# Attention-and-ternary-layer kernel on eight cores: another order of the lead-in, another order in the steps without Q/K jobs, and the last tile's products in other PSUM banks

## The reference, cut to what matters

```python
xn = layernorm(x)                                  # x: 2 x 16384 x 1024, no gain or bias
q, k, v = xn @ w_q + b_q, xn @ w_k + b_k, xn @ w_v + b_v          # 16 heads of 64
scores = einsum('bhsd,bhskd->bhsk', q, k_win) / 8  # window of 7 rows around each row
attn = softmax(scores masked to valid rows)
a = einsum('bhsk,bhskd->bhsd', attn, v_win) @ w_o + b_o
scale = max(mean(|weight|), 1e-5); wt = clip(round(weight / scale), -1, 1)
out = x + a + einsum('bsi,oi->bso', xn, wt * scale)
```

## Time and profile before

| | us |
|---|---|
| median of 3 runs | 704.99 (704.03 to 753.69) |
| the profiled execution | 706.46 |
| its span on core 3, the slowest | 704.9 |
| spans of the eight cores | 695.1 to 704.9 |
| busy time of PE on core 3 | 646.4 (92% of the span) |

### The profile page before, as it was taken

How to read it: one execution, slowest core, us unless ns; L and a number is a source line. 1 busy time by engine, 2 the same in 40 slices (tenths; PEclk the granted TensorE clock), 3 DMA queues, 4 the chain that set the end, 5 groups by cost and what they waited for, 6 DMA issues and landing times.

```text
span 704.9 us, 11682 instructions; the slowest of 8 cores (695.1 to 704.9 us)
## 1 busy us (share of the span) xinstructions
PE 646.4 (92%) x3890; PEld 300.0 (43%) x3890; DVE 435.1 (62%) x533; ACT 374.7 (53%) x1418; POOL 89.0 (13%) x52
## 2 busy tenths in 40 slices
PE   1669894989999999999999999999899999999996
PEld 1234341334444444444444444444344444555542
DVE  6135579476666666666665666666666655566662
ACT  3343366355555555555555555555555555556671
POOL 1013000231111111111111111001011111111200
PEclk9989997899999999999999999999899999999998
DMA  6989975657544454566553555554453432243322
GB/s 155 214 127 326 156 123 144 128 166 180 137 126 119 127 121 128 127 127 149 129 136 90 150 135 135 135 138 117 104 95 92 110 85 80 70 135 117 91 70 81
DMA packets 129803, 91.19 MB, mean 129 GB/s; under 512 B 107856, under 2 KB 116176, under 8 KB 129744
## 3 DMA queue, kind: packets, MB, share of 16 engines
q1 hardware_dynamic: 121296, 82.05, 44.9%
q0 software_dynamic: 8448, 8.39, 8.7%
HBM read 55.82 MB, written 16.78 MB: 103 GB/s over the span
## 4 chain that ended last, share of the span: by engine, by line
PE 81%; DVE 6%; DMA 4%; ACT 4%; issue 3%; POOL 1%; SPq 0%; DVEq 0%; ACTq 0%; POOLq 0%
PE p_p L301 16%; PE p_f L457 15%; PE p_p L283 15%; PE p_f L444 15%; PE p_p L326 14%; PE p_a L414 3%; DMA wq_b<-wq 3%; PE p_s L354 3%; ACT sm L384 3%; DVE sm L369 1%; DMA x<-x 1%; DVE nmx L376 1%; DVE xr L474 1%; DVE bst L204 1%; DVE xn L225 1%
## 5 line engine op out<-in xcount | busy, mean ns | idle before, releaser
L384 ACT ACTIVATE sm<-sm,nmx 122x128 f32<-122x128 f32 x544 | 210.7, 392 | 30.1 <-DVE nmx L376 30.1
L469 POOL TENSOR_TENSOR xr<-xr,brow 128x1024 f32<-128x1024 f32 x32 | 76.7, 2399 | 522.9 <-DMA xr<-x 456.1
L283 PE MATMUL p_p<-xnt,wq_b 128*128 128x488 bf16 (+1 forms) x576 | 128.1, 370 | 7.0 <-DMA wq_b<-wq 5.8
L301 PE MATMUL p_p<-xnt,wk_b 128*128 128x494 bf16 (+1 forms) x576 | 126.0, 366 | 0.0
L326 PE MATMUL p_p<-wv_b,xnt 128*128 128x512 bf16 x544 | 124.8, 383 | 0.0
L291 ACT ACTIVATE qt<-p_p,bq 128x488 bf16<-128x488 f32 (+1 forms) x72 | 46.4, 645 | 141.9 <-PE p_p L283 141.8
L444 PE MATMUL p_f<-wft_b,xnt 128*128 128x512 bf16 x512 | 119.5, 388 | 2.2 <-DVE xr L474 2.2
L457 PE MATMUL p_f<-wo_b,att 128*128 128x512 bf16 x512 | 116.5, 379 | 0.0
L384 ACT ACTIVATION_READ_ACCUMULATOR sm<-sm,nmx 122x1 f32 x544 | 104.6, 192 | 0.0
L369 DVE TENSOR_TENSOR sm<-p_s,mk_sb 122x1024 f32<-122x1024 f32 x68 | 82.9, 1219 | 30.0 <-PE p_s L354 30.0
L339 ACT CAST v<-p_p 128x512 bf16<-128x512 f32 x68 | 39.0, 574 | 98.8 <-PE p_p L326 98.8
(11 more groups left out here) (54 smaller groups left out, 267.2 us busy)
## 6 DMA issues: line engine op xcount, KB each, us to landing
xr<-x SPq DMA_DIRECT2D x32, 512.0 KB, 4.6
out<-xr SPq DMA_DIRECT2D x32, 512.0 KB, 3.3
x<-x SPq DMA_DIRECT2D x31, 512.0 KB, 4.3
wq_b<-wq POOLq DMA_DIRECT2D x4, 512.0 KB, 11.8
wk_b<-wk POOLq DMA_DIRECT2D x4, 512.0 KB, 11.9
xr<-wft SPq DMA_DIRECT2D x4, 512.0 KB, 10.5
wv_b<-wv POOLq DMA_DIRECT2D x4, 512.0 KB, 14.8
wo_b<-wo POOLq DMA_DIRECT2D x4, 512.0 KB, 24.9
```

The lines of the kernel that those rows point to most:

```text
L283: q.do("tensor", lambda e, k=k: e.matmul(bank[:, 0:m], w_b["wq"][:, k * H + 128 * c:k * H + 128 * c + 128], rows_of(b, k, BQ * b + 3, m), ...
L301: q.do("tensor", lambda e, k=k: e.matmul(bank[:, 0:m], w_b["wk"][:, k * H + 128 * c:k * H + 128 * c + 128], rows_of(b, k, BQ * b, m), star ...
L384: q.do("scalar", lambda e, h=h: e.activation(sm[hf][0:TQ, KW * h:KW * h + KW], sm[hf][0:TQ, KW * h:KW * h + KW], AF.Exp, bias=nmx[hf][0:TQ ...
L469: q.do("gpsimd", lambda e: e.tensor_tensor(xr[t % NR][:, :], xr[t % NR][:, :], brow[:, :], ALU.add), ("xrb", t))
```

## The change

`p_t` becomes two buffers (the second in `p_f`), used in turn. w_q's half 0 is issued in two parts, one after x tile 1 and one after x tile 2, and w_q's half 1 only after tile 6, ahead of w_k. The Q jobs of columns 4 to 7 of block 0 go behind those of columns 0 to 3 of block 1. `wf_scale` and the first terns go behind `k_job(1, 1)`; the exponentials of window 0 are spread otherwise over the K jobs, and `weights(0, 1)` is written behind window 0's V jobs. In steps that aren't `qk`, `output_step` (out_add and store) comes between the two mask additions and `layer_norm_step` (normalise, DMA transpose, x load) behind them, and `exps(n, 0)` and `weights(n, 0)` come behind `att_evict(s, 0)`. In step 0 the loads of `brow` and `xr` go behind both `e_transpose`s. The last tile's products go to `p_s`, its `o_proj` finishes column half 0 four matmuls before half 1, and each half is added and stored by itself.

```diff
-        p_t = p_a[:, :].bitcast(BF16)
+        p_t = [p_a[:, :].bitcast(BF16), p_f[:, 0:512].bitcast(BF16)]
...
         def xn_by_pe(r, *blocks):
             q.need("tensor", ("xn", r), "idm")
-            if t_last:
-                q.need("tensor", t_last[-1])
+            if r >= 2:
+                q.need("tensor", t_last[r - 2])
...
+        def p_out(t):
+            return p_s if t == NO - 1 else p_f
...
         def f_proj(t):
-            if t >= 1:
+            if t == NO - 1:
+                q.need("tensor", ("sadd", NW - 1, 1))
+            elif t >= 1:
                 q.need("tensor", ("out", t - 1))
...
         def o_proj(t):
+            order = [(k, jh) for k in range(8) for jh in range(2)]
+            if t == NO - 1:
+                order = [(k, jh) for kh in range(2) for jh in range(2) for k in range(4 * kh, 4 * kh + 4)]
...
-            q.need("tensor", "wsum")
+            q.need("tensor", "wsum", t_last[7])
...
-        q.need("gpsimd", ("x", 2))
-        weight_load("wq", 0)
-        weight_load("wq", 1)
+        q.need("gpsimd", ("x", 1))
+        weight_load("wq", 0, (0,))
+        q.need("gpsimd", ("x", 2))
+        weight_load("wq", 0, (1,))
         q.need("sync", ("w", "wq", 0))
         x_load(4)
...
         q.need("gpsimd", ("x", 6))
+        weight_load("wq", 1)
         weight_load("wk", 0)
         weight_load("wk", 1)
         xn_by_pe(3, 0, 1)
-        for c in range(8):
+        for c in range(4):
             q_job(0, c)
-            if c in (3, 5, 6, 7):
-                r = {3: 4, 5: 5, 6: 6, 7: 7}[c]
-                stats(r)
-                rstd(r)
-                normalise(r)
-                if r >= 5:
-                    xn_by_pe(r - 1, 1)
+            if c >= 1:
+                stats(3 + c)
+                rstd(3 + c)
+                normalise(3 + c)
+            if c >= 2:
+                xn_by_pe(2 + c, 1)
+        stats(7)
+        rstd(7)
+        normalise(7)
+        xn_by_pe(6, 1)
         xn_by_pe(7, 1)
...
-        for c in range(8):
-            q_job(1, c)
+        for b, c in ([(1, c) for c in range(4)] + [(0, c) for c in range(4, 8)]
+                     + [(1, c) for c in range(4, 8)]):
+            q_job(b, c)
         for c in range(8):
             k_job(0, c, "scalar")
-            if c == 6:
-                wf_scale()
-                some_terns(0, 2)
         scores(0, 0)
         mask_max(0, 0)
         k_job(1, 0, "scalar")
+        k_job(1, 1, "scalar")
+        wf_scale()
+        some_terns(0, 2)
         scores(0, 1)
         mask_max(0, 1)
         some_terns(2, 4)
...
         for s in range(NW):
...
+            if qk or n == NW:
+                output_step(s)
+                layer_norm_step(s)
...
                 scores(n, 0)
                 mask_max(n, 0)
                 v_job(n, 0)
                 v_evict(n, 0)
-                exps(n, 0)
+                if qk:
+                    exps(n, 0)
                 v_job(n, 1)
                 v_evict(n, 1)
+                if not qk:
+                    output_step(s)
                 scores(n, 1)
                 mask_max(n, 1)
+                if not qk:
+                    layer_norm_step(s)
+            if t is not None and t + 2 < NO and t >= 1:
+                xr_load(t + 2)
+            if t is not None and t >= 1:
+                xr_bias(t)
             if after is not None:
                 stats(after)
-            if n < NW:
+            if qk and n < NW:
                 weights(n, 0)
-            if s == 0:
-                late_terns()
             att_v(s, 0)
             att_evict(s, 0)
+            if not qk and n < NW:
+                exps(n, 0)
+                weights(n, 0)
             if n < NW:
                 e_transpose(n, 0)
             if t is not None:
                 f_proj(t)
+            if s == 0:
+                some_terns(6, 8)
...
-        out_add(NO - 1)
-        store(NO - 1)
+        t = NO - 1
+        for jh in range(2):
+            cols = slice(512 * jh, 512 * jh + 512)
+            q.need("vector", ("oh", t, jh), ("xrb", t))
...
+            q.dma("sync", f"o{t % NR}", lambda e, cols=cols: e.dma_start(
+                out_h[KW * t:KW * t + KW, cols], xr[t % NR][:, cols]), ("st", t))
```

More of the change, by code:

```diff
@@ L159, in rows_of, with weight_load @@
             return xnt[b % 3][:, lo:lo + n]
-        def weight_load(n, half):
+        def weight_load(n, half, parts=(0, 1)):
             cols = slice(512 * half, 512 * half + 512)
-            for k in range(2):
+            for k in parts:
                 q.dma("gpsimd", f"{n}{half}", lambda e, k=k: e.dma_start(
@@ L450, in o_proj @@
             i = out_step(t)
+            acc = p_out(t)
             q.need("tensor", ("w", "wo", 0), ("w", "wo", 1), ("att", i, 0))
-            for k in range(8):
-                if k == 4:
+            order = [(k, jh) for k in range(8) for jh in range(2)]
+            if t == NO - 1:
+                order = [(k, jh) for kh in range(2) for jh in range(2) for k in range(4 * kh, 4 * kh + 4)]
+            for k, jh in order:
+                if (k, jh) == (4, 0):
                     q.need("tensor", ("att", i, 1))
                 lo = k * AR + KW * t % AR
[L456 to L460, removed]
+                q.do("tensor", lambda e, k=k, jh=jh, lo=lo: e.matmul(
+                    acc[:, 512 * jh:512 * jh + 512], att[:, lo:lo + KW],
+                    w_b["wo"][:, k * H + 512 * jh:k * H + 512 * jh + 512],
+                    start=False, stop=(k == 7)), ("oh", t, jh) if k == 7 else None)
+            q.point[("o", t)] = q.point[("oh", t, 1)]
         def xr_load(t):
@@ L626, in build_program @@
         v_evict(0, 1)
+        weights(0, 1)
         e_transpose(0, 0)
@@ L635, in stats_of_step, with layer_norm_step, output_step @@
             return r if b < NB and r <= last_tile(b) else None
-        def late_terns():
-            some_terns(6, 8)
-            q.need("sync", "wft")
-            q.dma("sync", "bo", lambda e: e.dma_start(brow[:, :], bo_h[:, :]), "bo")
-            xr_load(0)
-            xr_load(1)
+        def layer_norm_step(s):
+            b, r = 2 + s // BW, stats_of_step(s)
+            if r is not None:
+                if s == 0:
+                    stats(r)
+                    rstd(r)
+                normalise(r)
+                if s % BW == 0:
+                    xn_by_dma(b, r - 1)
+                xn_by_dma(b, r)
+                if r + NX < NL:
+                    x_load(r + NX)
+        def output_step(s):
+            before = tile_of.get(s - 1)
+            if before is not None:
+                out_add(before)
+                store(before)
         for s in range(NW):
@@ L703, in build_program @@
                 e_transpose(n, 1)
+            if s == 0:
+                q.need("sync", "wft")
+                q.dma("sync", "bo", lambda e: e.dma_start(brow[:, :], bo_h[:, :]), "bo")
+                for k in range(3):
+                    xr_load(k)
             if t == 0:
```

45 lines of the change are left out of this document (16 added, 29 removed).

## The result

The changed kernel takes 695.83 us (median of 4 runs, 695.24 to 696.35). The ratio to the kernel before is 0.9876, 95% interval 0.9853 to 0.99: 8.7 us of 705. The time lies inside the range of 688.5 to 697.0 but 3.8 us above the forecast, and the largest part of what is missing is one term, the lead-in. An execution of any kernel here can take 721 us and more, the cores of one die then showing a lower granted clock; such executions are in none of the ratios.

The account below looks back on a forecast made before the run. PE was taken to bound steps 4 to 31, a block that only moves; gains lay before and behind: 1.7 + 4.6 + 3.4 + 4.7 = 14.4 us off 706.46 gave 692.1, forecast 692.0 us, range 688.5 to 697.

Parts of the forecast that it names:

- Part 1: Lead-in up to the first K job: K jobs start at 63.3 instead of 65.0 us, a gain of 1.7 us.
- the late core's excess is already in my lead-in term: Reason for not also subtracting the 1.5 us by which the median lies under the profiled execution.
- the term for the two transpose buffers: Lead-in chain from x tile 4's landing to block 1's first Q job: 0.9 us off, 15.1 instead of 16.0 us.
- the chain starts when tile 4 lands: Lead-in: x tile 4 lands at 26.2 us, and block 1's first Q job starts 15.1 us later, at 41.3 us.
- x tile 4 lands over 6 us after its issue: Lead-in sign that the forecast is wrong; the forecast itself took 4.4 us for this landing.
- first rival: Lead-in: x tiles don't land sooner since all cores load at once; everything moves by 4.3 us, 696.3 us; chance 0.13.
- Parts 2 and 3: Steps 0 and 1 gain 4.6 us with DVE the bound; steps 2 and 3 gain 3.4 us at 12.7 us each.
- sum of DVE's stretch: Steps 0 and 1: DVE's 42.9 us up to window 2's scores becomes 37.8 us, so these come at 118.3 us.
- Part 4: Tail from step 32 to the end: 4.7 us won, 3.75 of it up to O's end.
- The 0.95 us for the halves: End of the tail: a half add of 0.64 instead of 1.28 us and a half store of 2.4 instead of 2.7.
- w_v was never late: Rival that weights land late, up to window 0's second V job: all gain gone at 3.4 us a piece; chance 0.03.
- the rival priced: Rival that the wait moves to ACT and DVE: steps 2 and 3 stay at 14.3 us, 695.3 us; chance 0.11.

Follow-up runs that it names:

- experiment 1: Changed kernel with loads and Q job order of before, two transpose buffers kept: 695.13 us, ratio 0.9853 to the kernel before.
- experiment 7: Changed kernel with w_q's half 1 right behind half 0, still issued in two parts, and the Q jobs in the order of before: 692.69 us.
- experiment 9: Kernel before with only the loads, transpose buffers and Q order of the change: 706.25 us, ratio 1.001.
- experiment 3: Changed kernel with the loop's order of before in the steps, new lead-in and tail kept: 704.04 us, ratio 0.9977 to the kernel before.
- experiment 2: Changed kernel with the scale and first terns back behind K job (0, 6): 694.38 us, ratio 0.9836 to the kernel before.
- experiment 4: Changed kernel with the last tile's products back in `p_f`, one add and one store: 698.76 us, ratio 0.9901 to the kernel before.
- experiment 6: Changed kernel with one add and one store for the last tile, products still in `p_s`, `o_proj` in its usual order: 694.81 us, ratio 0.9855.
- experiment 8: As experiment 7, but x tiles 4 to 7 not held for w_q, and tiles 4 and 5 normalised ahead of the first Q job: 689.43 us.
- experiment 11: Experiment 8 plus the scale behind K job (0, 6), a single last store, and tile 8 normalised in DVE's idle gap behind `k_job(0, 3)`: 682.58 us.

## Why the prediction was right and wrong

**Part 1 failed**, and with it the sum's sentence that "the late core's excess is already in my lead-in term". The term was worked out as the gain of core 3: 49.59 to 41.3 us for block 1's first Q job is 8.3 us, less 6.6 for four jobs moved behind. On core 3 it came out so (8.05 us, K jobs 2.0 us earlier). But 49.59 was the latest of eight cores; the average was 46.4 before and is 41.1 after, 5.2 us earlier, while the jobs behind it take 22.0 us instead of 15.3. The average core loses 1.4 us, and the metric follows the latest core: 65.00 before, 66.23 after.

On that core, against the forecast's 63.3, x tile 4 was issued 0.7 us earlier and took 2.3 us longer, the chain behind it took 0.9 us more and the twelve jobs 0.3. The 0.9 us is the term for the two transpose buffers, and it didn't come on any core: the shortest way from DVE's start on tile 4 to block 1's first Q job is 15.98 us in the changed kernel, 15.99 before. The term's own low end, "nothing, since DVE's own part is serial", is what was measured. And that the chain starts when tile 4 lands was wrong on five cores, where ACT's wait for a Q job ahead of `rstd(4)` made it 16.5 to 18.3 us.

Core 1's row stood ready, 47.64 us: with it the term would have been 47.64 − 41.3 − 6.6 = −0.3. Experiments 1, 7 and 9 show it: undoing the lead-in costs nothing, a different one is 3.1 us better, and the new one alone takes 0.7 us more than the kernel before beside it (ratio 1.001). Of the mark set for being wrong, "x tile 4 lands over 6 us after its issue", core 5's 6.7 us is the case. That is the forecast's first rival halfway (it priced a landing of 8.7 us, 696.3 us in all), with the other half of the loss in the jobs moved behind.

The stretches, as forecast and as measured (us, changed kernel less the one before; the slowest cores are 3 before and 5 after):

| | forecast | slowest core | mean of the cores |
|---|---|---|---|
| to the first K job | −1.7 | +1.2 | +1.4 |
| K jobs to step 4 | −8.0 | −6.9 | −6.3 |
| step 4 to step 32 | 0 | −1.3 | −0.5 |
| step 32 to the last matmul | −3.75 | −3.5 | −3.5 |
| last matmul to the end | −0.95 | +0.3 | −0.5 |
| sum | −14.4 | −10.1 | −9.3 |

The slowest core is 4.3 us short of the forecast: 2.9 for the lead-in, 1.3 for the half stores, 1.1 for the steps and 0.3 between step 32 and the last matmul, less 1.3 us that came off between steps 4 and 32, where nothing was changed: luck.

**Parts 2 and 3 were right in the main.** Forecast were 8.0 us on core 3 from the K jobs to step 4, and 0.75 more where the new order frees O in step 32; experiment 3 measured 8.2 us, and core 3 itself 7.3 (from 65.00 and 166.96 to 62.96 and 157.58: 101.96 less 94.62). DVE is the bound in steps 0 and 1, with two idle stretches of PE at the forecast places; steps 2 and 3 take 25.2 us (forecast 25.3), and lose 0.65 at `att_evict` and 0.45 at `out_add` (forecast 0.3 to 0.5 and 0.4). A slip of 0.3 us lies in the sum of DVE's stretch: 42.9 less the terms named, plus 1.2, is 38.1 and not 37.8. On cores 1, 2 and 7 steps 2 and 3 take 26.0 to 26.7 us, mostly for a reason that the sum has no term for: in step 3 PE waits 0.73 to 1.41 us for the DMA transposes of `en`. What the part missed is that one of its edits works against it. It let the scale start 3.4 us later (80.5 us) with the words that "DVE is the bound", and did not ask what an idle DVE ahead of its own chain costs: 2.7 us on the path (experiment 2).

**Part 4 was right up to the last matmul**: 3.5 us on core 3 against 3.75. By experiments 3 and 4 the banks alone would give 3.1 of it, the order in step 32 alone 2.2. The 0.95 us for the halves came on core 3 (3.30 instead of 4.47 us from the last matmul to the end) and didn't come on the slowest core (4.78). The halves land after 2.1 us on core 3 and 3.1 on core 5; the forecast said 2.4, and the Trainium skill ("DMA: Bandwidth & Descriptors", the anatomy of one DMA on the gpsimd path) leads, as an estimate, to 2.6 for a half and 3.2 for a whole. The rule's point, that halving doesn't halve, agrees with these: a whole store took 2.7 us before and 3.1 in experiment 6, a half 2.1 or 2.9 to 3.4.

**The other rivals.** w_v was never late: no V job of windows 0 or 1 waits for a DMA. In steps 2 and 3 ACT and DVE hold PE for 1.1 us in all, not for the 3.2 us that the rival priced.

**The balance of the experiments**, from the medians: steps −8.2, tail −2.9, lead-in alone +0.7, and the scale's new place +1.4 (experiment 2). Together −9.0 us, against 8.7 by the ratio. That they come so close is luck. By the means of the spans the same four are −7.8, −3.0, +1.4 and +2.6, together −6.8 of some 9.3 us. Each has an interval of 0.8 to 2 us either way, and the steps' order and the banks overlap in step 32, so that undoing one at a time misses part of what they bring together.

## What to carry to other kernels

Where cores start the same work at different times, work out a term once on the latest core and once on an ordinary one: what removes one core's bad luck isn't a gain of the kernel. Moving work behind a chain to make the chain start earlier pays only if its end moves by more than that work on the core that comes last; starting the chain earlier without holding other loads back (experiment 8) gave more. Read the chain on every engine in it: a tile that lands early gains nothing if the next step of its chain stands behind other work in an engine's list. And when an engine is the bound of a stretch, look at its idle time ahead of that stretch: moving one piece of work into it gave 2.7 us on the path in experiment 2 and 4.8 us of the time in experiment 11.

## What the runs showed of the hardware

- The last two stores of 256 KB land after 2.1 us on one core and 3.1 on another of the same run, and the end of PE to the end of the span is 3.2 to 5.2 us over the cores of the changed kernel, where it was 4.45 to 4.52 before. In experiment 3 the halves take 2.1 us on all eight cores, in experiments 7 and 8 on none (3.1 to 3.4). What decides it, nothing here explains.
- From step 4 to step 32, where the change moves nothing, core 3 takes 508.6 us in both kernels, core 0 of the changed kernel only 507.1 and core 2 only 505.8; values within 0.5 us of these three come back in the kernels above, on changing cores. The difference is in step 21, which has no output tile: PE waits 3.2 us for `att_evict` on all three, and the clock granted around it differs. The stretch of 480 to 500 us on cores 0, 2 and 3 (columns as in the earlier trace rows):

```profile
480.00:500.00 20.00, 16.48 (x104) 7.58 (x104) 13.10 (x17) 10.74 (x42) 0.00 (x0) 0.91 0.46 99
...
480.00:500.00 20.00, 16.79 (x111) 7.81 (x110) 13.53 (x17) 10.81 (x41) 0.00 (x0) 1.00 0.46 108
...
480.00:500.00 20.00, 16.80 (x98) 7.28 (x97) 11.66 (x15) 10.91 (x41) 0.00 (x0) 0.83 0.46 98
```

  The same pause of 3.2 us costs 0, 1.3 or 2.8 us of slow matmuls behind it, a granted clock of 1.00, 0.91 or 0.83. Which of them a core gets isn't set by the pause's length alone; what sets it stays open. F of the last tile in experiment 4 shows the same: after a wait of 1.19 to 1.20 us it takes 5.30 us on core 3 and 3.61 on core 2. The spread of 2.8 us is larger than the forecast's whole term for the lead-in (1.7), and a single profiled execution doesn't average it out.
- In experiment 8 x tiles 3 and 4, which go to `sm`, landed 9.2 us after their issue (median) beside w_q, where tile 4 took 6.7 us on core 5 of the changed kernel and 3.4 to 5.1 on the others, and the kernel was still 6.4 us faster: an early start won over a quick transfer. Beside w_q's half 1, in the kernel before, tile 4 took 8.2 to 9.7 us over the eight cores.
